# Gated cross attention kernel: three PSUM banks for scores and one for all that follows the turned weights, in place of two and two

## Chip, cores and metric

One core of one Trainium2 chip. The time is the device time of one execution in microseconds (us), the median of the runs shown. Engines are called PE (matrix multiplication), DVE (vector), ACT (scalar), POOL (GpSimd) and SP (here only the queue that issues transfers). PEld is the loading of weights into PE, which can overlap PE's streaming.

## What is computed

A block of a transformer for 32 batches of 100 tokens of width 256, each with its own context of 361 tokens. The change touches only the first half, the cross attention:

```python
Q, K, V = LN(x) @ Wq.T + bq, ctx @ Wk.T + bk, ctx @ Wv.T + bv     # 16 heads of 16
attn = softmax(mask(Q K^T / 4))                                   # 100 x 361 per head
O = concat(attn @ V) @ Wo.T + bo
x = x + tanh(g_xattn) * O
```

The second half (self attention whose values and outputs are mixed from 8 experts per head) follows, and takes 1,320 us of the 1,873.

## The kernel before

The program runs in three stretches. The queries of all batches come first (to 57 us), then the cross attention (57 to 551 us), then the second half. The cross attention is `stage_cross` (L396): each engine has its own program there, with the same frame. `batches` (L82) calls `body(b)` for each of the 32 batches: two written out, 26 in a hardware loop of two batches a turn (even batch first), and four written out at the end. `body` has 16 **steps**, one per head. In each step an engine issues its own work for the step's head, and, lagging behind, work for heads of earlier steps; at the start of a body those are still heads of the batch before (`lagging`, L413). Nothing is reordered at run time: an engine issues in exactly this order, and stops at a wait until the semaphore has the value.

For a head h of batch b:

- PE, step h, `scores` (L887): one matmul of 361 columns into a bank of `c_ps`. It waits until DVE has read the scores that the bank held before (L891).
- DVE, step h, `masked` (L682): adds the mask, writes `c_sm` to SBUF and finds the maximum. L689 is this and its read of the accumulator.
- ACT, step h, `exp` (L800, L805).
- PE, step h+4, `turn` (L895, L899): three transposes into a bank of `c_pt`.
- DVE or (for six heads of 16) ACT, step h+5 or h+4, `copy_ext` (L694, L699; L825, L830): PSUM to SBUF.
- PE, step h+6, for four heads at once, `attend` (L903, L920): 24 products of weights and values. So these come at steps 9 and 13 (heads 0 to 3 and 4 to 7 of this batch) and 1 and 5 (heads 8 to 11 and 12 to 15 of the batch before). They write columns 0 to 199 of a bank of `c_pa`.

Then, for the batch before, in the body of b: DVE `invert` (step 2, L701), POOL `spread` (L598), PE `turn_rden` (step 6, L927: denominators turned into columns 256 to 455 of the same bank of `c_pa`), ACT `copy_rt` (step 7, L809, L812: those columns to SBUF), DVE `normalize` (step 9, L706, L710: sums times denominators into `c_an`), PE `project` (steps 14 and 15, L935, L938: `c_an` times the output weights into columns 0 to 255 of the same bank). And for the batch before that one, DVE `residual` (step 0, L712, L719), `moments` (step 1) and `mean_var` (step 2); SP stores the result. In the last batch `project` stands at steps 11 and 12 (`behind_last`, L965) and the three operations of DVE at steps 12 to 14 (L768). PE also computes keys for two batches ahead (L864; steps 0, 2, 3, 4) and values for the next (L881; steps 6 to 12), in two banks of `c_pp`.

All eight banks of PSUM are used: two each for `c_ps`, `c_pt`, `c_pa` and `c_pp`. The bank of `c_pa` is that of the batch's parity, so sums of one batch collect in one while the batch before is normalized and projected in the other. The only wait for it at `attend` is L909: that `residual` of two batches earlier has read its bank.

Of the kernel before, what the change touches and what calls it, by code (L numbers as in the profile page):

```python
# [395 lines left out]
def stage_cross(nc, k, sems, queries, cross, f, x, ctx_t, mask, q_parts, k_parts, big, mv, x1, sel_t, q_t, k_t):  # L396
# [10 lines left out]
    LAG_T, LAG_C, LAG_E, LAG_A = 4, 5, 4, 6  # L407
    RING = 2 * CLOSE
    RT = 256
    ACT_COPIES = (1, 4, 7, 10, 13, 15)  # L410
    TAIL = 12

# [7 lines left out]
    with ExitStack() as ctx:  # L420
# [15 lines left out]
        an = m.sbuf("c_an", [P, DC * SQ])  # L436
        x1s, xt = (m.sbuf(f"c_x1{n}", [SQ, 2, D]) for n in "st")
        warm = m.sbuf("c_warm", [P, 1])
        p_s = m.psum("c_ps", [P, 2, 512])
        p_t = m.psum("c_pt", [P, 2, 512])  # L440
        p_a = m.psum("c_pa", [P, 2, 512])
        p_p = m.psum("c_pp", [P, 2, 512])
        s_one, s_bvb, s_bo, s_tg = (held.sem(f"c_s_{n}") for n in ("one", "bvb", "bo", "tg"))
        s_ctx, s_kwh, s_kwl, s_kst, s_qst, s_mask, s_x, s_st = (
# [221 lines left out]
        def vector_programs(dve):  # L666
            def bias_values():
                dve.memset(ones[:, :], 1.0).then_inc(s_one, 1)
                dve.wait_ge(s_one, 1)
                dve.wait_ge(queries.s_weights, 48)  # L670
                for c in range(DC):
                    dve.tensor_scalar(bvb[:, c, :], ones[:, :], bvc[:, c:c + 1], None,
                                      ALU.mult).then_inc(s_bvb, 1)

            def key_lo(b, c):
                dve.wait_ge(s_khi, DC * b.n + c + 1)
                at_least(dve, s_kwl[b.par], 16 * b.half)
                dve.scalar_tensor_tensor(out=klo[:, b.par, c, :], in0=p_p[:, c, 0:SK],
                                         scalar=bkc[:, c:c + 1], in1=khi[:, b.par, c, :],
                                         op0=ALU.add, op1=ALU.subtract).then_inc(s_klo, 1)  # L680

            def masked(b, h):  # L682

                if h == 0:
                    dve.wait_ge(s_mb, b.n + 1)
                dve.wait_ge(s_s, XH * b.n + h + 1)
                at_least(dve, s_ex, XH * b.n + h - 3)
                pass_wait(dve, s_pass_dve)
                dve.tensor_tensor_reduce(  # L689
                    out=sm[:, h % 4, :], in0=p_s[0:SQ, h % 2, 0:SK], in1=mbias[:, b.par, :],  # L690
                    scale=-0.25 / WS, scalar=BIG, op0=ALU.add, op1=ALU.min,
                    accum_out=nmax[:, h % 4:h % 4 + 1]).then_inc(s_sm, 1)

            def copy_ext(b, h):  # L694
                if h in ACT_COPIES:
                    return
                dve.wait_ge(s_t, XH * b.n + h + 1)
                at_least(dve, s_pv, XH * b.n + h + 1 - RING)
                dve.tensor_copy(ext[:, h % RING, :], p_t[0:KW, h % 2, 0:KC * SQ]).then_inc(s_extd, 1)  # L699

            def invert(b):  # L701
                dve.wait_ge(s_ex, XH * (b.n + 1))
                at_least(dve, s_rdx, b.n)
                dve.reciprocal(rden[:, :], den[:, b.par, :]).then_inc(s_rd, 1)

            def normalize(b):  # L706
                dve.wait_ge(s_pv, XH * (b.n + 1))
                dve.wait_ge(s_rt, b.n + 1)
                at_least(dve, s_o, b.n)
                dve.tensor_tensor(an[:, :], p_a[:, b.par, 0:DC * SQ], rt[:, :], ALU.mult).then_inc(s_an, 1)  # L710

            def residual(b):  # L712
                dve.wait_ge(s_o, b.n + 1)
                dve.wait_ge(s_xb, b.n + 1)
                if not leaves(b):
                    dve.wait_ge(s_kept, b.n + 1)
                    dve.wait_ge(s_st[b.par], 16 * (b.half + 1))
                    pass_wait(dve, s_pass_dve)
                dve.scalar_tensor_tensor(out=x1_at(b), in0=p_a[0:SQ, b.par, 0:D],  # L719
                                         scalar=k.tanh_g[0:SQ, 0:1], in1=xbias[:, b.par, :],  # L720
                                         op0=ALU.mult, op1=ALU.add).then_inc(s_x1, 1)

            def moments(b):
                dve.wait_ge(s_x1, b.n + 1)
                at_least(dve, s_mv, b.n)
                pass_wait(dve, s_pass_dve)
                dve.bn_stats(st[:, :], x1_at(b)).then_inc(s_bn, 1)

            def mean_var(b):
                dve.wait_ge(s_bn, b.n + 1)  # L730
                if not leaves(b):
                    dve.wait_ge(s_kept, b.n + 1)
                pass_wait(dve, s_pass_dve)
                dve.bn_aggr(moments_at(b), st[:, :]).then_inc(s_mv, 1)

            def start(n):
                if n in (0, 3):
                    for c in range(DC):
                        key_lo(fixed(n // 3), c)
                elif n == 4:  # L740
                    bias_values()
                elif n == 6:
                    dve.wait_ge(s_bo, 1)
                    dve.wait_ge(queries.s_tanh, 1)
                    dve.tensor_scalar(tgbo[:, :], p_p[:, 0, 0:D], k.tanh_g[:, 0:1], None,
                                      ALU.mult).then_inc(s_tg, 1)

            def tail(b, step):
                if step == 0:
                    residual(b)  # L750
                if step == 1:
                    moments(b)
                if step == 2:
                    mean_var(b)

            def body(b):
                for i in range(XH):
                    lagging(b, i, LAG_C, copy_ext)
                    masked(b, i)
                    if i in (3, 5) and later(b, 2):  # L760
                        key_lo(later(b, 2), i // 5)
                    if i == 2 and not is_first(b):
                        invert(b.before())
                    if i == 9 and not is_first(b):
                        normalize(b.before())
                    if has_two_before(b):
                        tail(b.before().before(), i)
                    if is_last(b):  # L768
                        tail(b.before(), i - 12)

            def rest():
                batches(dve, body)
                last = fixed(NB - 1)
                for i in range(XH, XH + LAG_C):
                    lagging(last, i, LAG_C, copy_ext)
                invert(last)
                normalize(last)
                residual(last)
                moments(last)
                mean_var(last)  # L780

            return start, rest

        def scalar_programs(act):
# [24 lines left out]
            def copy_rt(b):  # L809
                act.wait_ge(s_r, b.n + 1)  # L810
                at_least(act, s_an, b.n)
                act.activation(rt[:, :], p_a[:, b.par, RT:RT + DC * SQ], ACT.Copy).then_inc(s_rt, 1)  # L812

            def start(n):
                if n in (0, 3):
# [40 lines left out]
        def tensor_programs(pe):  # L856
# [30 lines left out]
            def scores(b, h):  # L887
                if h == 0:
                    pe.wait_ge(s_kst[b.par], 64 * (b.half + 1))
                    pe.wait_ge(s_qst[b.par], 128 * (b.half + 1))  # L890
                at_least(pe, s_sm, XH * b.n + h - 1)  # L891
                pe.matmul(p_s[0:SQ, h % 2, 0:SK], qst[:, b.par, HEAD[h], :], kst[:, b.par, HEAD[h] // 2, :],  # L892
                          start=True, stop=True).then_inc(s_s, 1)

            def turn(b, h):  # L895
# [7 lines left out]
            def attend(b, h):  # L903
# [2 lines left out]
                first = h - CLOSE + 1  # L906
                if first == 0:
                    pe.wait_ge(s_vz, KC * (b.n + 1))
                    at_least(pe, s_x1, b.n - 1)  # L909
                mine = range(first, h + 1)  # L910
                for by_act in (False, True):
                    copied = [n for n in mine if (n in ACT_COPIES) == by_act]
# [2 lines left out]
                for c in range(KC):  # L915
                    for n in range(first, h + 1):
                        head = HEAD[n]
                        row, col, odd = 32 * (head % XG // 2), SQ * (head // XG), head % 2
                        v = vz[:, b.par, c, head // 2, :, :].rearrange("p a d -> p (a d)")
                        last = pe.matmul(p_a[row:row + 32, b.par, col:col + SQ],  # L920
                                         v[:, XD * odd:XD * odd + 32],
                                         ext[:, n % RING, c * SQ:(c + 1) * SQ],
                                         start=odd == 0 and c == 0, stop=odd == 1 and c == KC - 1)
# [2 lines left out]

            def turn_rden(b):  # L927
                pe.wait_ge(s_rdx, b.n + 1)
                for c in range(DC):
                    src = rdx[:, c * XG:(c + 1) * XG, :].rearrange("p h d -> p (h d)")  # L930
                    last = pe.transpose(p_a[:, b.par, RT + c * SQ:RT + (c + 1) * SQ], src,
                                        k.ident[0:SQ, 0:SQ])
                last.then_inc(s_r, 1)

            def project(b, c):  # L935
                if c == 0:
                    pe.wait_ge(s_an, b.n + 1)
                last = pe.matmul(p_a[0:SQ, b.par, 0:D], an[:, c * SQ:(c + 1) * SQ], wo[:, c, :],  # L938
                                 start=c == 0, stop=c == DC - 1)
                if c == DC - 1:  # L940
                    last.then_inc(s_o, 1)
# [20 lines left out]
            ahead = {0: (2, keys, 0, 0), 2: (2, keys, 0, 1), 3: (2, keys, 1, 0), 4: (2, keys, 1, 1),  # L962
                     6: (1, values, 0, 0), 7: (1, values, 0, 1), 8: (1, values, 1, 0), 10: (1, values, 1, 1), 11: (1, values, 2, 0), 12: (1, values, 2, 1)}
            behind = {6: (turn_rden,), 14: (project, 0), 15: (project, 1)}
            behind_last = {6: (turn_rden,), 11: (project, 0), 12: (project, 1)}  # L965

            def body(b):
                for i in range(XH):
                    scores(b, i)
                    if i in ahead and later(b, ahead[i][0]):  # L970
                        n, work, *args = ahead[i]
                        work(later(b, n), *args)
                    owed = behind_last if is_last(b) else behind
                    if i in owed and not is_first(b):
                        work, *args = owed[i]
                        work(b.before(), *args)
                    lagging(b, i, LAG_T, turn)
                    lagging(b, i, LAG_A, attend)
# [1009 lines left out]
```

## Time and profile before

| | |
|---|---|
| median of 3 runs | 1874.32 us (1874.13 to 1876.52) |
| the profiled execution's own time | 1874.45 us |
| its span, first to last instruction | 1872.7 us |
| PE busy | 1839.2 us (98%) |
| PEld busy | 1136.9 us (61%) |
| DVE busy | 1469.4 us (78%) |
| ACT busy | 1124.4 us (60%) |
| POOL busy | 1067.1 us (57%) |
| granted TensorE clock | 0.997 of full speed |

The 1.7 us between the span and the execution's time lie outside the first and last instruction. The shares are averages over the whole program; the change is in the stretch from 57 to 551 us only. Ends of matmuls are modelled in this profile (a matmul is shown with its whole latency, and the next may start before the shown end), so starts are the numbers to compare.

### The profile page before, as it was taken

How to read it: one execution, taken by the hardware profiler on the slowest of the kernel's cores; microseconds unless marked ns; L12 is line 12 of the kernel's file. 1: busy time of each engine (PE TensorE's matmuls, PEld its weight loads, DVE VectorE, ACT ScalarE, POOL GpSimd, SP SyncE). 2: the span in 40 equal slices, each digit the busy share in tenths (PEclk: the TensorE clock that was granted, in tenths of full speed). 3: DMA queues.
4: the chain of work that ended last, by engine and by line, in shares of the span. 5: the costliest groups of instructions: out<-in, count | busy, mean ns of one | idle time of the engine just before them, and what ended most of it. 6: DMA issues, size and time to landing. Idle time of an engine off the chain costs nothing. (4 is left out here: it accounts for less than half of the span.)

```text
span 1872.7 us, 57738 instructions
## 1 busy us (share of the span) xinstructions
PE 1839.2 (98%) x13454; PEld 1136.9 (61%) x13454; DVE 1469.4 (78%) x4212; ACT 1124.4 (60%) x3581; POOL 1067.1 (57%) x1722
## 2 busy tenths in 40 slices
PE   6999999999989999999999999999999999999998
PEld 4788888888876554444444445555555555555543
DVE  7799999999979725555555566679999999999989
ACT  4799989998975454444444455455555555555543
POOL 4144444466730005666666666666766776767766
PEclk9999999999999999999999999999999999999999
DMA  5555555565414762000000032122222222222201
GB/s 174 154 128 129 131 125 123 124 160 135 119 32 177 279 249 89 28 28 28 14 28 28 28 121 63 55 79 77 69 78 74 67 82 72 68 82 73 68 25 56
DMA packets 161975, 174.24 MB, mean 93 GB/s; under 512 B 49905, under 2 KB 148594, under 8 KB 159858
## 3 DMA queue, kind: packets, MB, share of 16 engines
q1 hardware_dynamic: 159730, 165.05, 30.2%
q0 software_dynamic: 2176, 8.39, 1.2%
q8 instruction: 28, 0.46, 0.1%
q14 instruction: 41, 0.34, 0.1%
HBM read 112.41 MB, written 60.98 MB: 93 GB/s over the span
## 5 line engine op out<-in xcount | busy, mean ns | idle before, releaser
L1608 POOL TENSOR_TENSOR o_side<-o_side,o_tmp 128x256 f32 (+1 forms) x528 | 397.4, 753 | 190.2 <-POOL o_side L1608 73.4
L1369 PE MATMUL e_pv<-e_vw,e_xhi 128*128 (+1 forms) x1600 | 475.9, 379 | 0.0
L1299 ACT ACTIVATE big<-e_pv,gates 128x128 f32<-128x128 f32 x800 | 227.9, 368 | 279.4 <-PE e_pv L1369 277.9
L1736 ACT ACTIVATE o_tmp<-o_py,gates 128x256 f32<-128x256 f32 x528 | 221.9, 474 | 193.1 <-PE o_py L1808 134.1
L805 ACT ACTIVATE c_ex<-c_sm,c_nmax 100x361 f32<-100x361 f32 x512 | 302.4, 594 | 33.4 <-DVE c_nmax L689 22.3
L1808 PE MATMUL o_py<-o_whi,a_chi 128*128 128x512 f16 x800 | 303.9, 380 | 1.1 <-issue 0.6
L1369 PE MATMUL e_pv<-e_vw,e_xlo 128*128 (+1 forms) x800 | 303.2, 379 | 0.0
L1808 PE MATMUL o_py<-o_whi,a_clo 128*128 128x512 f16 x800 | 303.1, 379 | 0.0
L1808 PE MATMUL o_py<-o_wlo,a_chi 128*128 128x512 f16 x800 | 303.0, 379 | 0.0
L689 DVE CUSTOM_DVE_ANT_0 c_sm<-c_ps,c_mbias 100x361 f32<-100x361 f32 x512 | 270.1, 529 | 34.3 <-PE c_ps L892 27.6
L1244 DVE TENSOR_SCALAR e_acc<-e_pv,gates 128x128 f32<-128x128 f32 x400 | 121.8, 346 | 221.4 <-PE e_pv L1369 221.3
L1668 DVE SCALAR_TENSOR_TENSOR o_main<-o_py,gates,o_main 128x256 f32 (+1 forms) x536 | 256.2, 478 | 36.9 <-issue 22.2
L1369 PEld LDWEIGHTS e_pv<-e_vw,e_xhi 128*128 (+1 forms) x1600 | 156.6, 98 | 185.1
L1668 DVE SCALAR_TENSOR_TENSOR o_side<-o_py,gates,o_side 128x256 f32 (+1 forms) x536 | 254.4, 475 | 0.0
L1146 POOL TENSOR_TENSOR big<-big 128x256 f32<-128x256 f32 x200 | 144.6, 723 | 169.8 <-ACT big L1299 169.5
L899 PE MATMUL c_pt<-ident,c_ex 100*121 100x100 f32 x1536 | 237.4, 264 | 1.8 <-DVE c_ext L699 1.1
L899 PEld LDWEIGHTS c_pt<-ident,c_ex 100*121 100x121 f32 x1536 | 219.0, 185 | 16.6 <-issue 2.3
L892 PE MATMUL c_ps<-c_kst,c_qst 128*100 128x361 f16 x512 | 168.3, 329 | 1.3 <-DVE c_nmax L689 0.6
L699 DVE COPY c_ext<-c_pt 121x300 f32<-121x300 f32 x320 | 148.0, 463 | 8.4 <-PE c_pt L899 6.6
L1719 ACT ACTIVATE a_ex<-a_ps,a_mxs 100x100 f32<-100x100 f32 x256 | 84.5, 342 | 103.9 <-DVE a_mxs L1639 97.4
L1369 PEld LDWEIGHTS e_pv<-e_vw,e_xlo 128*128 (+1 forms) x800 | 78.3, 98 | 94.4
L1808 PEld LDWEIGHTS o_py<-o_whi,a_clo 128*128 (+1 forms) x800 | 78.1, 98 | 94.7
(172 smaller groups left out, 3240.1 us busy)
## 6 DMA issues: line engine op xcount, KB each, us to landing
qk<-e_out SPq DMA_DIRECT2D x16, 1600.0 KB, 5.2
c_kst<-k_parts SPq DMA_DIRECT2D x128, 180.5 KB, 3.4
a_q<-qk SPq DMA_DIRECT2D x64, 200.0 KB, 2.4
a_k<-qk SPq DMA_DIRECT2D x64, 200.0 KB, 2.5
v<-e_out SPq DMA_DIRECT2D x20, 640.0 KB, 3.3
a_v<-v SPq DMA_DIRECT2D x64, 200.0 KB
c_ctx<-in_ctx_t SPq DMA_DIRECT2D x32, 361.0 KB, 3.6
e_wst<-in_v_w POOLq DMA_DIRECT2D x8, 1024.0 KB, 8.4
```

The source lines that it names most:

```text
L689: dve.tensor_tensor_reduce(out=sm[:, h % 4, :], in0=p_s[0:SQ, h % 2, 0:SK], in1=mbias[:, b.par, :], scale=-0.25 / WS, scalar=BIG, op0=ALU. ...
L699: dve.tensor_copy(ext[:, h % RING, :], p_t[0:KW, h % 2, 0:KC * SQ]).then_inc(s_extd, 1)
L805: act.activation(ex[:, h % 4, 0:SK], sm[:, h % 4, :], ACT.Exp, scale=-1.0, bias=nmax[:, h % 4:h % 4 + 1], accum_out=den[:, b.par, HEAD[h]: ...
L892: pe.matmul(p_s[0:SQ, h % 2, 0:SK], qst[:, b.par, HEAD[h], :], kst[:, b.par, HEAD[h] // 2, :], start=True, stop=True).then_inc(s_s, 1)
L899: last = pe.transpose(p_t[0:KW, h % 2, c * SQ:(c + 1) * SQ], ex[:, h % 4, c * KW:(c + 1) * KW], k.ident[0:SQ, 0:SQ])
L1146: pool.tensor_tensor(tsum[:, hh, :, :], tmp[:, hh, 0:2, :], tmp[:, hh, 2:4, :], ALU.add).then_inc(s_ts, 1)
L1299: act.activation(tmp[:, hh, e, :], p_v[:, hh, 1, e * PD:(e + 1) * PD], ACT.Copy, scale=gate).then_inc(s_av, 1)
L1369: last = pe.matmul(p_v[:, hh, half, :], a[:, c, bass.ds(t * P, P)], vw[:, bass.ds(col + (w * DC + c) * VW, 512)], start=j == 0, stop=j == ...
L1608: pool.tensor_tensor(side[:, x.t, :], side[:, x.t, :], tmp[:, slot(x, r), j, :], ALU.add).then_inc(s_pool, 1)
L1668: dve.scalar_tensor_tensor(out=into[:, x.t, :], in0=p_y[:, q, j, :], scalar=gate, in1=into[:, x.t, :], op0=ALU.mult, op1=ALU.add).then_inc ...
L1736: act.activation(tmp[:, slot(x, r), j, :], p_y[:, q, j, :], ACT.Copy, scale=gate).then_inc(s_av, 1)
L1808: last = pe.matmul(p_y[:, q, :, :].rearrange("p j d -> p (j d)"), a[:, bass.ds(buf * T + x.t * P, P)], b[:, buf, cut], start=j == 0, stop= ...
```

## The change

`c_ps` gets a third bank and `c_pa` keeps one. Heads go to banks 0, 1, 2, 0, 1, 2, ... and at the end of a batch 0, 1, 2, 1. A score matmul waits for the earlier head with its bank, which is three heads back in most places, two at heads 1 and 15, four at heads 0 and 2. With one bank for all of `c_pa`:

- sums stay in columns 0 to 199 and turned denominators in 256 to 455; the projection moves to columns 256 to 511.
- `attend` of heads 0 to 3 (step 9) waits until `normalize` of the batch before is done (`s_an`); `normalize` moves from DVE's step 9 to its step 8.
- `attend` of heads 8 to 11 (step 1 of the next body) waits until `residual` of the batch before its own is done (`s_x1`). That `residual` stands at step 0 of the same body. `turn_rden` gets the same kind of wait.
- in the last batch, `project` goes back to steps 14 and 15, and DVE's three operations for batch 30 move behind the body, between the last copies.

```diff
+    BANK = (0, 1, 2) * 4 + (0, 1, 2, 1)
+    BACK = tuple(next(d for d in range(1, XH) if BANK[h - d] == BANK[h]) for h in range(XH))
...
-        p_s = m.psum("c_ps", [P, 2, 512])
+        p_s = m.psum("c_ps", [P, 3, 512])
         p_t = m.psum("c_pt", [P, 2, 512])
-        p_a = m.psum("c_pa", [P, 2, 512])
+        p_a = m.psum("c_pa", [P, 512])
...
-                dve.tensor_tensor(an[:, :], p_a[:, b.par, 0:DC * SQ], rt[:, :], ALU.mult).then_inc(s_an, 1)
+                dve.tensor_tensor(an[:, :], p_a[:, 0:DC * SQ], rt[:, :], ALU.mult).then_inc(s_an, 1)
...
-                dve.scalar_tensor_tensor(out=x1_at(b), in0=p_a[0:SQ, b.par, 0:D],
+                dve.scalar_tensor_tensor(out=x1_at(b), in0=p_a[0:SQ, RT:RT + D],
...
-                    if i == 9 and not is_first(b):
+                    if i == 8 and not is_first(b):
                         normalize(b.before())
                     if has_two_before(b):
                         tail(b.before().before(), i)
-                    if is_last(b):
-                        tail(b.before(), i - 12)
...
                 for i in range(XH, XH + LAG_C):
                     lagging(last, i, LAG_C, copy_ext)
+                    tail(last.before(), i - XH)
...
-                at_least(pe, s_sm, XH * b.n + h - 1)
-                pe.matmul(p_s[0:SQ, h % 2, 0:SK], qst[:, b.par, HEAD[h], :], kst[:, b.par, HEAD[h] // 2, :],
+                at_least(pe, s_sm, XH * b.n + h + 1 - BACK[h])
+                pe.matmul(p_s[0:SQ, BANK[h], 0:SK], qst[:, b.par, HEAD[h], :], kst[:, b.par, HEAD[h] // 2, :],
...
                 if first == 0:
                     pe.wait_ge(s_vz, KC * (b.n + 1))
-                    at_least(pe, s_x1, b.n - 1)
+                    at_least(pe, s_an, b.n)
+                if first == 2 * CLOSE:
+                    at_least(pe, s_x1, b.n)
...
             def turn_rden(b):
                 pe.wait_ge(s_rdx, b.n + 1)
+                at_least(pe, s_x1, b.n)
...
-                last = pe.matmul(p_a[0:SQ, b.par, 0:D], an[:, c * SQ:(c + 1) * SQ], wo[:, c, :],
+                last = pe.matmul(p_a[0:SQ, RT:RT + D], an[:, c * SQ:(c + 1) * SQ], wo[:, c, :],
...
-            behind_last = {6: (turn_rden,), 11: (project, 0), 12: (project, 1)}
```

The reads and writes of `c_ps` and `c_pa` that are not shown change their bank index in the same way.

## Rows read from the trace of the kernel before

**Rows 1.** Busy time by stretch: from:to, length, engine busy (x instructions), clock, DMA

```profile
102.00:117.00 15.00, 15.00 (x196) 13.03 (x195) 13.59 (x49) 13.57 (x44) 9.97 (x24) 1.00 0.51 128
525.00:540.00 15.00, 14.30 (x178) 11.88 (x178) 13.33 (x51) 13.34 (x44) 5.98 (x19) 1.00 0.03 8
```

**Rows 2.** Groups of instructions, 72 to 512 us: busy, mean ns | idle before

```profile
L689 DVE CUSTOM_DVE_ANT_0 c_sm<-c_ps,c_mbias 100x361 f32<-100x361 f32 x460 | 243.2, 529 | 30.0 <-PE c_ps L892 23.8 <-issue 0.2
...
L892 PE MATMUL c_ps<-c_kst,c_qst 128*100 128x361 f16 x460 | 151.0, 328 | 0.0
...
L920 PE MATMUL c_pa<-c_ext,c_v 121*32 121x100 f32 x2764 | 83.4, 253 | 0.0
...
L892 PEld LDWEIGHTS c_ps<-c_kst,c_qst 128*100 128x100 f16 x460 | 57.6, 125 | 17.4 <-DVE c_nmax L689 11.5 <-issue 5.9
```

**Rows 3.** Timeline, batch 16, steps 4, 5 and scores of 6, 10: start, length

```profile
304.11 0.32 PE L892 MATMUL c_ps<-c_kst,c_qst 128*100 128x361 f16 x1
...
305.02 0.32 PE L892 MATMUL c_ps<-c_kst,c_qst 128*100 128x361 f16 x1
...
305.57 0.72 PE L920 MATMUL c_pa<-c_ext,c_v 121*32 121x100 f32 x24
...
306.22 0.12 PEld L892 LDWEIGHTS c_ps<-c_kst,c_qst 128*100 128x100 f16 x1 [0.15 <-issue]
...
310.02 0.12 PEld L892 LDWEIGHTS c_ps<-c_kst,c_qst 128*100 128x100 f16 x1 [0.15 <-DVE c_nmax L689]
```

**Rows 4.** Timeline, batch 16, from PE's step 6 to its step 9

```profile
306.92 0.48 PE L899 MATMUL c_pt<-ident,c_ex 100*121 100x100 f32 x3
...
307.52 0.47 DVE L699 COPY c_ext<-c_pt 121x300 f32<-121x300 f32 x1 [0.18 <-PE c_pt L899]
...
308.09 0.32 ACT L812 ACTIVATE c_rt<-c_pa 128x200 f32<-128x200 f32 x1
...
308.36 0.47 DVE L699 COPY c_ext<-c_pt 121x300 f32<-121x300 f32 x1
...
308.74 0.53 DVE L689 CUSTOM_DVE_ANT_0 c_sm<-c_ps,c_mbias 100x361 f32<-100x361 f32 x1
...
309.34 0.54 DVE L689 CUSTOM_DVE_ANT_0 c_sm<-c_ps,c_mbias 100x361 f32<-100x361 f32 x1
...
309.37 0.72 PE L920 MATMUL c_pa<-c_ext,c_v 121*32 121x100 f32 x24
...
309.80 0.36 DVE L710 TENSOR_TENSOR c_an<-c_pa,c_rt 128x200 f32<-128x200 f32 x1
```

**Rows 5.** Timeline, step 1 of PE in batches 16, 17; step 15 between

```profile
301.36 0.48 DVE L719 SCALAR_TENSOR_TENSOR c_x1s<-c_pa,tanh_g,c_xbias 100x256 f32<-100x256 f32 x1
...
301.59 0.72 PE L920 MATMUL c_pa<-c_ext,c_v 121*32 121x100 f32 x24
...
315.08 0.53 DVE L689 CUSTOM_DVE_ANT_0 c_sm<-c_ps,c_mbias 100x361 f32<-100x361 f32 x1 [0.34 <-PE c_ps L892]
...
316.48 0.48 DVE L719 SCALAR_TENSOR_TENSOR c_x1s<-c_pa,tanh_g,c_xbias 100x256 f32<-100x256 f32 x1
...
316.88 0.72 PE L920 MATMUL c_pa<-c_ext,c_v 121*32 121x100 f32 x24
```

**Rows 6.** Timeline, behind the last batch, where PE does wait

```profile
545.94 0.42 ACT L830 ACTIVATE c_ext<-c_pt 121x300 f32<-121x300 f32 x1 [1.04 <-PE c_pt L899]
...
546.51 0.72 PE L920 MATMUL c_pa<-c_ext,c_v 121*32 121x100 f32 x24 [0.60 <-ACT c_ext L830]
...
548.37 0.37 DVE L710 TENSOR_TENSOR c_an<-c_pa,c_rt 128x200 f32<-128x200 f32 x1 [2.11 <-issue]
...
548.79 1.11 PE L938 MATMUL c_pa<-c_w,c_an 128*100 128x256 f32 x4 [1.24 <-DVE c_an L710]
```

**Rows 7.** Timeline, behind the last batch: DVE

```profile
543.30 0.84 DVE L699 COPY c_ext<-c_pt 121x300 f32<-121x300 f32 x2
...
545.63 0.47 DVE L699 COPY c_ext<-c_pt 121x300 f32<-121x300 f32 x1 [1.48 <-PE c_pt L899]
```

More of the change, by code:

```diff
@@ L689, in masked @@
                 dve.tensor_tensor_reduce(
-                    out=sm[:, h % 4, :], in0=p_s[0:SQ, h % 2, 0:SK], in1=mbias[:, b.par, :],
+                    out=sm[:, h % 4, :], in0=p_s[0:SQ, BANK[h], 0:SK], in1=mbias[:, b.par, :],
                     scale=-0.25 / WS, scalar=BIG, op0=ALU.add, op1=ALU.min,
@@ L811, in copy_rt @@
                 at_least(act, s_an, b.n)
-                act.activation(rt[:, :], p_a[:, b.par, RT:RT + DC * SQ], ACT.Copy).then_inc(s_rt, 1)
+                act.activation(rt[:, :], p_a[:, RT:RT + DC * SQ], ACT.Copy).then_inc(s_rt, 1)
             def start(n):
@@ L919, in attend @@
                         v = vz[:, b.par, c, head // 2, :, :].rearrange("p a d -> p (a d)")
-                        last = pe.matmul(p_a[row:row + 32, b.par, col:col + SQ],
+                        last = pe.matmul(p_a[row:row + 32, col:col + SQ],
                                          v[:, XD * odd:XD * odd + 32],
@@ L928, in turn_rden @@
                 pe.wait_ge(s_rdx, b.n + 1)
+                at_least(pe, s_x1, b.n)
                 for c in range(DC):
                     src = rdx[:, c * XG:(c + 1) * XG, :].rearrange("p h d -> p (h d)")
-                    last = pe.transpose(p_a[:, b.par, RT + c * SQ:RT + (c + 1) * SQ], src,
+                    last = pe.transpose(p_a[:, RT + c * SQ:RT + (c + 1) * SQ], src,
                                         k.ident[0:SQ, 0:SQ])
@@ L972, in body @@
                         work(later(b, n), *args)
-                    owed = behind_last if is_last(b) else behind
-                    if i in owed and not is_first(b):
-                        work, *args = owed[i]
+                    if i in behind and not is_first(b):
+                        work, *args = behind[i]
                         work(b.before(), *args)
```

## The prediction

> **What bounds the kernel now.** I first read the busy time by stretch, to see which engine fills the stretch that the change touches. In a slice of 15 us inside the cross attention PE is busy for all 15.00 us, DVE for 13.59 and ACT for 13.57 [rows 1]. As a matmul's shown end is modelled, that alone doesn't prove that PE never waits. So next come the groups of instructions from 72 to 512 us: PE's idle time is 0.0 in front of the scores (L892) and of the sums (L920), while DVE was idle for 30.0 us in front of its masking, of which 23.8 waiting for scores from PE [rows 2]. DVE waits for PE; PE waits for nobody. Last, the timeline of one batch: the scores of steps 4 and 5 start at 304.11 and 305.02, 0.91 us apart [rows 3], and that is only the streaming of what stands between them (one score matmul, three for keys, three transposes). A batch takes 15.3 us on PE, set by PE's own instructions. The thing to carry over: whatever delays PE in this stretch adds to the time, and whatever relieves a wait of PE gains only if there was one.
>
> **The third bank for scores: no gain, 0 us.** It lets PE issue the scores of a head before DVE has read those of two heads back. One row looks like such a wait: PEld is idle for 17.4 us in front of the scores' weights, 11.5 of it put down to DVE's maximum (L689) and 5.9 to "issue" [rows 2]. But each of these gaps is the same 0.15 us whichever name it has, and each stands behind a group of sums: at 306.22 it is "issue", at 310.02 "DVE" [rows 3]. For the latter the masking that had to be done was that of head 8, started at 308.74 and over at 309.27 [rows 4], 0.75 us before the load at 310.02. A wait that had ended 0.75 us earlier holds nothing. The gap belongs to the switch from the narrow 32-column products to a full-width one; the edit doesn't touch it. The instructions are the same in number and size, so nothing is gained or lost by them either. The Trainium skill ("Perfetto Trace Analysis", section "Matmuls") says that independent groups of matmuls should rotate through different banks, so that the copying out of one overlaps the next. By that rule the scores could only gain, and the sums, which stop rotating, must lose; the two effects are weighed here by the rows, and in this kernel the rule speaks against the change.
>
> **The one bank for sums: a wait at step 9.** `attend` of heads 0 to 3 now needs `normalize` of the batch before. PE reaches it at 309.37 [rows 4]. The chain on DVE that leads there starts at PE itself: the transposes of step 6 start at 306.92; DVE, idle for 0.18 us until they are done, copies at 307.52; then come masking 7, the copy at 308.36, masking 8 at 308.74. The next operation behind a masking starts 0.46 us after it (309.34 to 309.80), so `normalize`, now at step 8, starts at 308.74 + 0.46 = 309.20. Its other input, ACT's copy of the denominators, is done by 308.09 + 0.32 = 308.41, so that doesn't hold it. It takes 0.36, to 309.56. From there to a matmul that waits for it: the last batch shows 548.37 + 0.37 = 548.74 and the matmul at 548.79, 0.05 us [rows 6]. So `attend` starts at 309.61 instead of 309.37: **0.24 us** lost. It can't be made up in the next batch, since the chain restarts each time from PE's own step 6; if PE is later, so is DVE. DVE has slack, but it lies in waits for PE, ahead of this chain. 31 batches have the wait: 31 x 0.24 = 7.4 us. Behind the waiting instruction the 24 products and then scores 10 are queued on PE; masking 10 on DVE and then exp on ACT wait for those and shift with them. `normalize` itself only changes places with masking 9: masking 9 goes from 309.34 to about 309.5, and PE asks for the bank of head 9 only at head 12 by the new order; ACT, which takes it next, has slack too (13.57 us busy of 15 [rows 1]). That costs nothing.
>
> **A wait at step 1.** `attend` of heads 8 to 11 now needs `residual`, which DVE issues at its step 0 of the same body. In an even batch `residual` starts at 301.36 and takes 0.48: 301.84, and with 0.05 for the signal 301.89, against 301.59 on PE: 0.30 us lost. In an odd one 316.48 + 0.48 + 0.05 = 317.01 against 316.88: 0.13 us [rows 5]. (DVE arrives later in even ones, which begin a turn of its loop.) Here too DVE comes from a wait for PE: 0.34 us in front of masking 15 at 315.08 [rows 5], so the loss recurs. Bodies 2 to 29 have it: 14 x 0.30 + 14 x 0.13 = 6.0 us. In bodies 30 and 31, without keys, PE has gaps of its own (14.30 us busy of 15 [rows 1]), and I count nothing. The wait of `turn_rden` at step 6 is for the same `residual`, five steps old: 0. Why the wait must be there though the columns differ: the Trainium skill ("PSUM — Partial Sum Buffer", section "PSUM bank collisions raise a hardware error") says that two engines may not be in the same bank and the same 32 partitions at once. No run here shows it; it only tells that the wait can't be dropped.
>
> **The last batch.** The two projections move from steps 11 and 12 to 14 and 15 on PE, and DVE's `residual`, statistics and mean of batch 30 move from steps 12 to 14 to behind the body. There DVE issues two copies at 543.30 and is then idle for 1.48 us until 545.63 [rows 7], which covers the three operations (`residual` takes 0.48 [rows 5], the two others I put at no more each). PE's chain at the end is copies and transposes. If the cover failed, the price would be at most the operations' own time, some 1.4 us. I take 0, between -0.5 and +1.4.
>
> **The sum.** 0 + 7.4 + 6.0 + 0 = 13.4 us on the profiled execution's 1874.45: 1887.9 us, 0.7% slower. The median of the runs is 0.1 below that execution, which changes nothing.
>
> **Bounds of the unknown costs.** No row shows these very waits. The signal takes 0.05 by the nearest row, the same operation of DVE followed by a matmul. The only sum that waits starts at 546.51, after an ACT copy that ends at 545.94 + 0.42 = 546.36: 0.15 us [rows 6]. With 0.15 for all 59 waits the loss grows by 59 x 0.10 = 5.9, to 1893.8. Downwards, records of starts may stand 0.1 us off the true order, which would take 5.9 off: 1882.0.
>
> **The rivals.**
> - *Only one wait bites.* If DVE is ahead of what the rows say at one place (its loop overhead in even batches shrinks, say), 7.4 or 6.0 us stay: 1880.5 to 1881.9. For: the odd gap is only 0.13. Against: both chains are released by PE. Chance 0.08.
> - *Faster: the scores' wait was real.* The place is PE's L892 behind a group of sums. If the gaps named after DVE in rows 2 were true waits on the reading of the bank, the third bank would take 11.5 us off; with the new waits hidden because DVE also gets the scores earlier, 1874.45 - 11.5 = 1863.0; it ends faster as long as the new waits cost under 0.19 us each (11.5 / 59). For: the name in the row. Against: all gaps are alike, and 0.75 us of slack. Chance 0.09. The skill's rule on rotation, read for the scores alone, would give this same time.
> - *No difference.* PE's starts in the trace are where its sequencer lets them go; if PE in truth is some 0.3 us behind the records when it comes to the sums, both waits are hidden: 1874.4. The same comes out if the waits were made without effect. For: PE's ends are modelled. Against: where DVE waits for PE, it starts right behind PE's shown end (306.92 + 0.48 = 307.40, the copy at 307.52 [rows 4]), which ties the records of the two engines together. Chance 0.09.
> - *The forecast*, both waits, 1882 to 1894: chance 0.74.
>
> **How the numbers follow.** 1887.9 is the forecast's own sum. From 1880 to 1894 the range takes the forecast and the first rival (0.82) and leaves out the other two. A change within 0.2% (3.7 us) is about what a measurement of this kernel can't tell from none. Faster 0.09, same 0.09, slower 0.82.
>
> **What would show it.** In the profile after: idle time of PE in front of L920 with the releaser `c_an` L710, some 31 times about 0.24 us, and with L719, some 28 times between 0.13 and 0.30; the batch period 15.7 to 15.8 us in place of 15.3; the PEld gap of 0.15 us in front of L892 still there, as often. DVE's idle in front of its masking grows by what PE loses. The second half is untouched in length. I am wrong if PE's idle in front of L920 stays near 0, if the gaps in front of L892 vanish, or if the waits are twice as long, which would mean that DVE doesn't come from a wait for PE.

## The result and the profile after

The changed kernel takes 1891.31 us (median of 5 runs, 1890.4 to 1891.43) against 1874.51 us (5 runs, 1874.13 to 1877.19) before. The ratio on record is 1.0079, with a 95% interval from 1.0068 to 1.0091: 0.7 to 0.9% slower. (It is not the quotient of the two medians, which is 1.0090 and lies inside the interval; the same holds for the ratios below.)

The head of the page of the changed kernel, its first two parts:

```profile
span 1889.6 us, 57783 instructions
PE 1843.7 (98%) x13454; PEld 1138.0 (60%) x13454; DVE 1468.9 (78%) x4212; ACT 1128.2 (60%) x3581; POOL 1067.7 (57%) x1722
```

The numbers of instructions on the engines are those of before, and so are their busy times to within 5 us. The span grew by 16.9 us, so the time went into gaps. Where they are is told by the groups of instructions of the changed kernel, from 72 to 512 us, which answer to [rows 2]:

```profile
L691 DVE CUSTOM_DVE_ANT_0 c_sm<-c_ps,c_mbias 100x361 f32<-100x361 f32 x446 | 235.7, 528 | 43.5 <-PE c_ps L893 24.0 <-ACT c_ex L806 13.1 <-issue 4.6
...
L893 PE MATMUL c_ps<-c_kst,c_qst 128*100 128x361 f16 x446 | 146.4, 328 | 0.0
...
L923 PE MATMUL c_pa<-c_ext,c_v 121*32 121x100 f32 x2688 | 80.9, 253 | 9.9 <-issue 5.6 <-DVE c_x1s L721 3.2
...
L923 PEld LDWEIGHTS c_pa<-c_ext,c_v 121*32 121x32 f32 x2688 | 56.9, 109 | 23.8 <-issue 9.7 <-DVE c_x1s L721 8.5
...
L893 PEld LDWEIGHTS c_ps<-c_kst,c_qst 128*100 128x100 f16 x446 | 55.9, 125 | 17.0 <-DVE c_nmax L691 8.6 <-issue 8.3
```

PE, which had no idle time in front of the sums before, now has 9.9 us there, and PEld 23.8 (11.3 before, where nothing was waited for). In front of the scores nothing changed: 0.0 for PE, and 17.0 for PEld where [rows 2] had 17.4. The name in that row moved from "DVE" towards "issue" and its sum stayed, which is what a gap looks like that is no wait. DVE's idle time in front of its masking grew from 30.0 to 43.5 us, which is about what PE loses in these batches. The names there say little: 13.1 us stand under ACT's exp here, and 3.5 in run 1 below, with the same total.

The timeline of one batch shows the wait at step 9. These rows of the changed kernel answer to [rows 4]:

```profile
316.39 0.53 DVE L691 CUSTOM_DVE_ANT_0 c_sm<-c_ps,c_mbias 100x361 f32<-100x361 f32 x1
...
316.61 0.48 PE L900 MATMUL c_pt<-ident,c_ex 100*121 100x100 f32 x3
...
316.84 0.36 DVE L712 TENSOR_TENSOR c_an<-c_pa,c_rt 128x200 f32<-128x200 f32 x1
...
317.31 0.33 PE L923 MATMUL c_pa<-c_ext,c_v 121*32 121x100 f32 x5 [0.21 <-issue]
```

`normalize` starts 0.45 us behind masking 8, as foretold. In the kernel before, the sums of this step started 0.41 us behind the start of the transposes, in the same batch:

```profile
308.96 0.48 PE L899 MATMUL c_pt<-ident,c_ex 100*121 100x100 f32 x3
309.37 0.72 PE L920 MATMUL c_pa<-c_ext,c_v 121*32 121x100 f32 x24
```

Here that would be 317.02, and they start at 317.31: 0.29 us lost. Two things are to be learnt from the row. The profile names the releaser "issue", not DVE, although the code has the wait on `s_an` there; and the idle time that it shows, 0.21, is not the loss, since a matmul's shown end is modelled. Starts against starts give the loss.

The wait at step 1, in PE's timeline of the changed kernel, an even batch and the next, odd one:

```profile
308.54 0.46 PE L900 MATMUL c_pt<-ident,c_ex 100*121 100x100 f32 x3
309.24 0.72 PE L923 MATMUL c_pa<-c_ext,c_v 121*32 121x100 f32 x24 [0.24 <-DVE c_x1s L721]
...
324.43 0.46 PE L900 MATMUL c_pt<-ident,c_ex 100*121 100x100 f32 x3
324.94 0.72 PE L923 MATMUL c_pa<-c_ext,c_v 121*32 121x100 f32 x24
```

At this step the distance before was 0.39 us (316.49 and 316.88 in its timeline). So 309.24 - 308.54 - 0.39 = 0.31 us are lost in the even batch, 324.94 - 324.43 - 0.39 = 0.12 in the odd one.

The prediction counted nothing in the last two batches, where no keys are computed. But they wait too. In batch 30 the sums start 530.11 - 529.35 = 0.76 us behind the transposes, where it was 515.71 - 515.25 = 0.46 before:

```profile
529.35 0.53 PE L900 MATMUL c_pt<-ident,c_ex 100*121 100x100 f32 x3
530.11 0.64 PE L923 MATMUL c_pa<-c_ext,c_v 121*32 121x100 f32 x20 [0.23 <-DVE c_x1s L721]
```

The same subtraction for all 128 groups of sums of the two traces gives, in total:

| where | batches | us each | us |
|---|---|---|---|
| step 9 (`normalize`) | 2 to 27 | 0.28 to 0.29 | 7.4 |
| step 9 | 1, 28, 29, 31 | 0.22 | 0.9 |
| step 9 | 30 | 0.49 | 0.5 |
| step 1 (`residual`) | 14 of batches 2 to 29 | 0.29 to 0.38 | 4.5 |
| step 1 | the other 14 | 0.11 to 0.13 | 1.8 |
| step 1 | 30 and 31 | 0.29 and 0.30 | 0.6 |
| steps 13 and 5 | all | 0 | 0.1 |

8.8 us at step 9 and 6.9 at step 1: 15.7 us.

Last, the change is in the first stretch only, so I compare where the second half begins: the first product of `e_pt`. Before, then after (the same lines in the two programs):

```profile
L1331 PE MATMUL e_pt<-ident,big x64: 249/256/397, 552.8 to 570.2; 100*128 100x100 f32 x64
```

```profile
L1333 PE MATMUL e_pt<-ident,big x64: 249/256/400, 568.4 to 586.4; 100*128 100x100 f32 x64
```

It begins 568.4 - 552.8 = 15.6 us later. The first scores start at 57.3 us before and 57.2 after. From there to the second half, which is the cross attention, it is 495.5 us before and 511.2 after: 15.7 us more, and that is what the waits give. Each experiment gives this length beside its time. (The first scores start anywhere from 57.1 to 59.5 us in the profiled executions of this study, with the same work ahead of them, so the start of the second half alone can mislead by up to 2 us. The five that start at 58.3 or later had the granted clock at 0.50 for 3.4 us between 23 and 29 us; in the other eight it stood at 1.00 there.)

The other 1.3 us of the span's growth lie in the second half, whose code is the same. It takes 1319.9 us before and 1321.2 after, and from 1318.0 to 1321.2 over the profiled executions of this study. A part of that is the granted clock. It falls to 0.50, the lower of its two levels (1.2 GHz), around where the second half begins (at 551.5 us before, at 564.9 after, at 562.6 in run 3 below). PE is idle for 1.24 us in front of the last projection there, for `normalize`, and for 2.90 us in front of the second half. How long the clock stays low differs from one execution to the next. The first 20 us of the second half, in the kernel before, the changed kernel and run 3 below (start and end, length, busy time of PE, PEld, DVE, ACT and POOL, clock, DMA):

```profile
552.80:572.80 20.00, 18.94 (x221) 16.88 (x222) 12.29 (x33) 14.56 (x57) 7.25 (x27) 0.86 0.30 107
```

```profile
568.40:588.40 20.00, 18.92 (x218) 17.14 (x219) 11.71 (x33) 14.56 (x57) 7.25 (x27) 0.83 0.29 107
```

```profile
562.40:582.40 20.00, 18.78 (x225) 16.26 (x226) 12.95 (x33) 15.07 (x58) 7.28 (x27) 0.91 0.29 107
```

The second halves of these three take 1319.9, 1321.2 and 1318.8 us.

### The profile page after: what moved, and what is told of

It is laid out like the page before. It is cut to its first block and busy times, and to the rows that moved or that the text cites. A ratio compares the mean times of both kernels' runs of the same rounds, so it can differ in the third digit from the quotient of the medians.

```text
span 1889.6 us, 57783 instructions
## 1 busy us (share of the span) xinstructions
PE 1843.7 (98%) x13454; PEld 1138.0 (60%) x13454; DVE 1468.9 (78%) x4212; ACT 1128.2 (60%) x3581; POOL 1067.7 (57%) x1722
```

## The experiments

All are built on the changed kernel, except where it says otherwise. The kernel before ran beside them on each chip, with medians of 1876.17 us (first four), 1874.85 (next four) and 1876.30 (last three).

**1. Is the third bank worth anything? Two banks for scores.**

```diff
-    BANK = (0, 1, 2) * 4 + (0, 1, 2, 1)
+    BANK = (0, 1) * 8
```

> The changed kernel with scores rotating over two banks only, not three (the third is left unused); one bank for sums as in the changed kernel. My theory (the third bank removes no wait): 1891 us, within 0.1% of the changed kernel, PE's idle in front of the sums as there. Rival (the third bank does bring something, and the new waits cost more than the net shows): slower than 1893 us, with PE idle in front of the scores.

Measured: 1890.08 us (1889.86 to 1890.38), ratio 1.0071 (1.0058 to 1.0085); cross attention 511.7 us. The changed kernel had 1.0079 and 511.2. Taking the third bank away changes nothing that can be measured. The PEld gap in front of the scores stays too:

```profile
L893 PEld LDWEIGHTS c_ps<-c_kst,c_qst 128*100 128x100 f16 x446 | 55.9, 125 | 17.0 <-DVE c_nmax L691 8.7 <-issue 8.3
```

**2. The wait at step 9 alone taken away: `normalize` ahead of masking 8.**

```diff
+                    if i == 8 and not is_first(b):
+                        normalize(b.before())
                     masked(b, i)
...
-                    if i == 8 and not is_first(b):
-                        normalize(b.before())
```

> The changed kernel with normalize issued ahead of masking 8 instead of behind it (DVE step 8). My theory: the wait of the sums at step 9 (0.31 us in the changed kernel) goes, 31 x 0.31 = 9.6 us, so 1881.7 us; the wait at step 1 stays. Rival (a pushed-back masking 8 delays exp and the transposes as much): 1891 us, with a new idle time in front of the transposes or scores.

Measured: 1882.02 us (1880.81 to 1883.92), ratio 1.0031 (1.0019 to 1.0043); cross attention 502.1 us, 9.1 less than in the changed kernel. The 9.6 expected came from a distance of 0.39 us before, where step 9 has 0.41. The sums' starts say that 8.8 us are those of step 9, and that the waits at step 1 lose 0.3 less. In front of the sums, the idle time of PE and PEld that is left is put down to DVE's `residual`:

```profile
L923 PE MATMUL c_pa<-c_ext,c_v 121*32 121x100 f32 x2736 | 82.4, 253 | 4.0 <-DVE c_x1s L721 3.2
...
L923 PEld LDWEIGHTS c_pa<-c_ext,c_v 121*32 121x32 f32 x2736 | 57.1, 109 | 17.1 <-DVE c_x1s L721 8.7
```

The whole "issue" part of the rows of the changed kernel (5.6 and 9.7) is gone, and with it the doubt about what that name stood for: it was the wait for `normalize`.

**3. The wait at step 1 alone taken away: `residual` ahead of masking 0.**

```diff
+                    if i == 0 and has_two_before(b):
+                        residual(b.before().before())
                     masked(b, i)
...
-                    if has_two_before(b):
+                    if i > 0 and has_two_before(b):
                         tail(b.before().before(), i)
```

> The changed kernel with residual issued ahead of masking 0 (DVE step 0). My theory: the wait at step 1 goes (0.31 in even bodies, 0.12 in odd ones, 28 bodies, 6.0 us, and up to 1 us more in the last two), so 1884.3 to 1885.3 us; the wait at step 9 stays. Rival (the wait only moves on to the next step, since masking 0 comes 0.4 us later): 1891 us.

Measured: 1882.95 us (1882.27 to 1885.05), ratio 1.0035 (1.0022 to 1.0049); cross attention 504.1 us, 7.1 less than in the changed kernel, so the 6.0 expected and the "up to 1 us more in the last two". (Its second half starts only 6.0 us sooner than the changed kernel's, but its first scores start 1.1 us later, at 58.3.) The time is below the 1884.3 to 1885.3 expected. In the profiled execution the second half was 2.4 us shorter than in the changed kernel, and 7.1 + 2.4 - 1.1 are the 8.4 us by which the span fell. What is left of PE's idle time in front of the sums is the other part:

```profile
L925 PE MATMUL c_pa<-c_ext,c_v 121*32 121x100 f32 x2712 | 81.6, 253 | 5.8 <-issue 5.5
```

**4. Both.** The edits of 2 and 3 together.

> Both reorderings of DVE together on the changed kernel. My theory (the whole loss is the two waits): 1874.5 to 1876 us, the time before the change, PE idle 0 in front of the sums, and no gain from the third bank. Rival (one bank for sums costs something of its own, or DVE's order matters): over 1878 us; rival (the third bank helps once the waits are gone): under 1872 us.

Measured: 1875.47 us (11 runs, 1874.37 to 1876.14), ratio 0.9994 (0.9985 to 1.0003); cross attention 495.9 us, 0.4 more than before. The kernel is back at the time of before, with one bank for sums:

```profile
L925 PE MATMUL c_pa<-c_ext,c_v 121*32 121x100 f32 x2760 | 83.1, 253 | 0.0
```

The order on DVE shows why. `normalize` now ends 0.28 us before the sums:

```profile
309.29 0.35 DVE L712 TENSOR_TENSOR c_an<-c_pa,c_rt 128x200 f32<-128x200 f32 x1
...
309.92 0.72 PE L925 MATMUL c_pa<-c_ext,c_v 121*32 121x100 f32 x24
```

So one bank for sums costs nothing of its own that can be measured; the two waits were the loss.

**5. Both, with two banks for scores.** The edits of 1 and 4.

> Both reorderings of DVE, and scores over two banks instead of three. My theory (the third bank is worth nothing even where no new wait stands): the time of both_first, 1874 to 1877 us. Rival (the third bank pays once the waits are gone): 2 us or more slower than both_first, with PE idle in front of the scores.

Measured: 1875.58 us (11 runs, 1874.29 to 1877.54), ratio 1.0002 (0.9993 to 1.0011); cross attention 495.7 us. The third bank is worth nothing where no new wait stands either: seven banks do what eight did.

**6. Both, with one bank for scores.**

```diff
-    BANK = (0, 1, 2) * 4 + (0, 1, 2, 1)
+    BANK = (0,) * 16
```

> Both reorderings of DVE, and scores in one bank only. It asks how many banks the scores need. Scores then wait for the masking of the head before, which ends some 1.1 us after those scores started (0.55 to its start, 0.53, and the signal), while a step of PE takes 0.78 to 1.2 us. My theory (the first to second bank is what counts): about 0.15 to 0.35 us lost in 12 of 16 steps, 3 us per batch, 1960 to 1990 us. Rival (PE's order hides even that): under 1880 us.

Measured: 2014.43 us (2 runs), ratio 1.0744 (1.0724 to 1.0763). The direction is right and the size expected was too small: the cross attention takes 633.9 us, 138 more than before. A batch of the loop takes 19.4 us in place of 15.3, so 4.1 more; in the last batch the granted clock was also at 0.50 for 17 us. In this kernel's timeline a step with values, which takes 0.78 us in the changed kernel, takes 1.18:

```profile
301.46 0.12 PEld L895 LDWEIGHTS c_ps<-c_kst,c_qst 128*100 128x100 f16 x1 [0.36 <-DVE c_nmax L691]
...
302.05 0.53 DVE L691 CUSTOM_DVE_ANT_0 c_sm<-c_ps,c_mbias 100x361 f32<-100x361 f32 x1
...
302.64 0.12 PEld L895 LDWEIGHTS c_ps<-c_kst,c_qst 128*100 128x100 f16 x1 [0.36 <-DVE c_nmax L691]
```

From the scores to the masking 302.05 - 301.46 = 0.59 us, the masking 0.53, the signal 0.06: 1.18, not 1.1. In the middle batches no step is shorter than that, so PE loses 0.40 us in those that took 0.78, where I had put 0.35 as the most. This is also what a true wait for a score bank looks like in the groups of this kernel. PE is idle too, and the PEld row has 98.3 us, to be set against the even 17 us of the others:

```profile
L895 PE MATMUL c_ps<-c_kst,c_qst 128*100 128x361 f16 x363 | 129.4, 356 | 39.0 <-DVE c_nmax L691 29.6
...
L895 PEld LDWEIGHTS c_ps<-c_kst,c_qst 128*100 128x100 f16 x363 | 43.9, 121 | 98.3 <-DVE c_nmax L691 97.4 <-issue 0.9
```

**7 and 8. What are the gaps around a group of sums? Eight heads at once.** First on the kernel before, then on the changed kernel (where the second wait has to be told the new group).

```diff
-CLOSE = 4
+CLOSE = 8
...
-                if first == 2 * CLOSE:
+                if first == XH // 2:
```

> The kernel before with the sums of eight heads at once, at steps 13 and 5 only, not of four at steps 9, 13, 1, 5 (and 16 buffers for the copies, not 8). It asks what the gaps around each group of sums are: in front of one PE is 0.09 us late, behind one PEld is idle for 0.15 us, with no waiting shown. My theory (they belong to the change between 32-column and full-width products, not to a wait): half of the groups go, 64 x 0.11 to 0.2 us, so 1862 to 1868 us. Rival (they are waits, or the double burst of 1.3 us starves DVE and ACT): 1875 us or slower.

> The changed kernel (three banks for scores, one for sums) with the sums of eight heads at once, at steps 13 and 5. The waits on normalize (step 8) and residual (step 0) then have four steps or more of slack, so by my theory this has no stall at the sums although the bank is one, and the time of close8_before; if the third bank matters under the double burst, up to some us less than close8_before. Rival (one bank costs something of its own): 10 us or more slower than close8_before.

Measured: 1884.39 us (1883.94 to 1886.32), ratio 1.0052 (1.0038 to 1.0065), and 1880.92 us (1880.21 to 1884.66), ratio 1.0036 (1.0022 to 1.005). Cross attention 508.5 and 502.4 us. What I expected of the time was wrong in both: slower than before, not 6 to 12 us faster. What I expected of the gaps was right. In the second of the two kernels, with half as many groups, PEld's idle time in front of the scores is half of what it was, and the name "DVE" is gone from it:

```profile
L893 PEld LDWEIGHTS c_ps<-c_kst,c_qst 128*100 128x100 f16 x454 | 57.4, 126 | 8.6 <-issue 7.9
```

So the gap goes with the groups of sums. The gain of it was given back by a new wait, in front of the transposes, where PEld had 11.7 us of idle time in the changed kernel:

```profile
L900 PEld LDWEIGHTS c_pt<-ident,c_ex 100*121 100x121 f32 x1363 | 190.0, 185 | 34.7 <-ACT c_ext L831 13.4 <-DVE c_ext L701 8.3 <-issue 1.1
```

While PE is at 48 products in a row, DVE has nothing to mask, and afterwards the copies of ACT and of DVE come too late for the transposes. DVE's and PEld's rows in the timeline of that kernel:

```profile
301.91 0.53 DVE L691 CUSTOM_DVE_ANT_0 c_sm<-c_ps,c_mbias 100x361 f32<-100x361 f32 x1 [0.81 <-PE c_ps L893]
```

```profile
305.29 0.39 PEld L900 LDWEIGHTS c_pt<-ident,c_ex 100*121 100x121 f32 x3 [0.36 <-DVE c_ext L701]
```

And here the waits of the single bank cost nothing, as they have several steps of slack: PE has 0.0 us of idle time in front of its sums, and the changed kernel is even 3.5 us faster than the kernel before, both with eight at once. In the loop a batch takes 15.50 us there against 15.64. (Of the 6.1 us between the two lengths above, a part is the clock: it fell to 0.50 9 us ahead of the second half in the first, 0.6 us ahead in the other.) That pair differs in the number of both kinds of banks, and no run takes the third bank away from the changed kernel with eight at once. Run 11 asks what the bank is worth in the next order only.

**9. The sums one place later: behind the scores of the next step.**

```diff
-    LAG_T, LAG_C, LAG_E, LAG_A = 4, 5, 4, 6
+    LAG_T, LAG_C, LAG_E, LAG_A = 4, 5, 4, 7
...
                     scores(b, i)
+                    lagging(b, i, LAG_A, attend)
...
                     lagging(b, i, LAG_T, turn)
-                    lagging(b, i, LAG_A, attend)
```

> The changed kernel with each group of sums issued one step later, right behind that step's scores (steps 10, 14, 2, 6; DVE's order as in the changed kernel). My theory: normalize (step 8) and residual (step 0) then are a whole step of PE earlier than the sums that wait for them, so both stalls go without any reordering of DVE: 1874 to 1877 us, PE idle 0 in front of the sums. Rival (PE is held elsewhere by the later sums): over 1878 us.

Measured: 1882.5 us (1881.88 to 1883.71), ratio 1.0032 (1.002 to 1.0045); cross attention 504.8 us, 9.2 more than before. Wrong, and the fault is mine: the sums stood at the end of a step, so behind the next step's scores is not a whole step later but one score matmul, 0.16 us. Taking 0.16 off the waits of 0.29 (step 9) and of 0.31 and 0.12 (step 1) leaves 0.13, 0.15 and nothing. In PE's timeline of this kernel, the sums behind the scores of step 2 (the wait for `residual`, even batch) and of step 10 (the wait for `normalize`):

```profile
305.18 0.32 PE L893 MATMUL c_ps<-c_kst,c_qst 128*100 128x361 f16 x1
305.58 0.72 PE L923 MATMUL c_pa<-c_ext,c_v 121*32 121x100 f32 x24
...
313.10 0.32 PE L893 MATMUL c_ps<-c_kst,c_qst 128*100 128x361 f16 x1
313.48 0.72 PE L923 MATMUL c_pa<-c_ext,c_v 121*32 121x100 f32 x24
```

The sums start 0.40 and 0.38 us behind the scores; where nothing waits it is 0.24 or 0.25 (309.30 to 309.54 in the same timeline). So 0.15 and 0.13 us are left, as the one matmul of delay says, and in odd batches the sums of step 2 start 0.25 us behind the scores: no wait. Over all batches 3.9 us are left at step 10 and 2.6 at step 2, 6.5 of the 9.2. Another 1.6 lie behind the last sums: from there to the second half it is 7.9 us (554.03 to 561.96) against 6.3 before (546.51 to 552.79), and the granted clock was at 0.50 for all of it:

```profile
554.00:562.00 8.00, 3.82 (x31) 2.25 (x32) 1.46 (x4) 1.82 (x3) 0.00 (x0) 0.50 0.05 14
```

The last 1.1 us, 0.04 per batch, aren't settled.

The run shows one thing more. With the sums right behind the scores, the PEld gap is gone from the scores and stands in front of what follows the sums now, mostly the values. So it goes with the place of the sums, not with the scores or their bank:

```profile
L893 PEld LDWEIGHTS c_ps<-c_kst,c_qst 128*100 128x100 f16 x453 | 57.4, 127 | 0.0
...
L882 PEld LDWEIGHTS c_pp<-c_whi,c_ctxhi 128*121 128x121 f16 x168 | 22.6, 134 | 8.5 <-issue 8.5
```

**10 and 11. Eight heads at once, behind that step's scores**, with three banks for scores and with two. The edits of 8 and 9, and for the second that of 1.

> The same with the sums of eight heads at once (steps 14 and 6, behind that step's scores). With eight at once the transposes were held by DVE's and ACT's copies, since DVE sat idle for 0.81 us in each burst. Now DVE has a head's scores to mask during the burst. My theory: the burst starves nobody, and the 64 groups saved give 64 x 0.11 = 7 us against the kernel before: 1867 to 1870 us. Rival (DVE, with 13.6 us of work in 15, can't follow uneven steps): 1875 us or slower.

> As ahead8, with scores over two banks and not three. If a third bank is worth anything in this kernel it is where DVE falls behind after a burst. My theory: 1 to 4 us slower than ahead8, as the two kernels with eight sums at once differed by 3.5 us. Rival: the same time.

Measured: 1882.87 us (1881.76 to 1886.79), ratio 1.0039 (1.0025 to 1.0053), and 1890.69 us (1890.47 to 1893.72), ratio 1.0083 (1.0069 to 1.0097). Cross attention 504.1 and 511.1 us. The first is no faster than run 8: one head's scores don't fill a burst of 1.2 us, and the transposes still wait for copies. The second answers the question of the third bank: here it is worth 7.0 us of the cross attention, 7.8 by the medians, and a batch of the loop takes 15.80 us in place of 15.55. Its list of waits (us in total, times, longest) has PEld waiting for DVE in front of the scores, which the first, with three banks, doesn't have:

```profile
PEld c_ps L893 <- DVE c_nmax L691: 5.6, 26, 0.2
PEld c_pp L882 <- DVE c_klo L680: 3.9, 26, 0.2
```

The second of these rows, in front of the values, looks like another cost of the missing bank and is none. With three banks the same gap is there, as long, under the name "issue":

```profile
PEld c_pp L882 <- issue: 4.2, 28, 0.2
```

It stands behind a group of sums in both. I had expected 1 to 4 us; the sign was right and the size too small.

## Why the prediction was right

It said 1887.9 us, from 1880 to 1894; measured are 1891.3. Point by point:

- *What bounds the stretch.* PE, without a wait. The experiments agree: with both waits gone the time is that of before, and nothing done to banks or to the order brought it below that.
- *Third bank: 0 us.* Right, by runs 1 and 5. The reason given, that the row naming DVE in front of the scores shows a fixed gap and no wait, is shown by run 8, where the gap halves with the groups, by run 9, where it moves with them, and by run 6, where a true wait looks different. The faster rival took that row at its word; it fell with these.
- *The wait at step 9: 7.4 us.* The mechanism was right; the size is 8.8 (0.29 instead of 0.24 in most batches). The term that was mis-sized is the signal from DVE to the waiting sums: 0.05 us was taken from `project` behind `normalize` in the last batch. Here it is 317.31 - 317.20 = 0.11 by these rounded rows, and 0.10 in all 31 batches. The upper bound, from the only sum that waits before, was 0.15, so the value lies between the two rows.
- *The wait at step 1: 6.0 us.* In the 28 batches that were counted the waits are 0.31 and 0.12 against 0.30 and 0.13, and make 6.3 us. Here the signal is 0.05 to 0.06. The step that failed, a small one, is to count nothing in the last two: PE's gaps of its own don't cover the wait there, 0.3 us are lost in each. With them it is 6.9, and run 3 took 7.1 off.
- *Last batch: 0.* It wasn't tried by itself. From the sums of its step 9 to its last sums it takes 9.13 us before (537.38 to 546.51), 9.27 in the changed kernel (552.61 to 561.88) and 9.27 also in run 4 without the waits, so moving the work there cost some 0.15 us.
- *The sum.* 13.4 foreseen, 15.7 in the cross attention: 1.4 more at step 9, 0.9 more at step 1. The other 1.1 of the 16.8 us between the medians is within what the second half scatters by, which no term of the sum was for.
- *What to look for.* The idle time in front of the sums, the batch period (15.8 us on average; batches of 15.7 and 15.9 us take turns) and the unchanged gap in front of the scores came as written. Not as written: the wait for `normalize` stands in the profile as "issue", and the one for `residual` is named 16 times in PE's rows, not 28, since a wait of 0.12 us leaves PE no idle time to show.
- *One bite only, no difference.* Runs 2 and 3 show that both waits bite: without them the cross attention is 9.1 and 7.1 us shorter.

That two engines may not be in one bank and the same 32 partitions at once was taken from the Trainium skill ("PSUM — Partial Sum Buffer", section "PSUM bank collisions raise a hardware error") to explain why the waits are there. No run here shows what happens without them.

## What to carry to other kernels

Where one engine is full and waits for nobody, a bank more for what it writes brings nothing, and a bank less costs what the waits cost that replace it. (Runs 10 and 11 are the other case: once that engine does wait for the reader of a bank, the bank counts.) So with a bank less, look for each such wait at what the other engine issues just before, and move that one instruction one place up. Here two such moves on DVE made seven banks as good as eight, and left one bank free. Whether a named wait is one is told by its size: the same length under two names, going with what stands in front, is the engine's own. And where a sum comes out, look at its terms one by one all the same. With 0.39 for 0.41 us at step 9, and nothing for the last two batches, the waits would make 9.6 + 6.0 = 15.6 us, the right total from two wrong terms.

## What was not expected

- A group of products that waits for DVE's `normalize` starts 0.10 us behind its shown end, in all 31 batches; one that waits for `residual`, 0.05 to 0.06, in every batch where it waits. Both are DVE operations in front of the same line of PE's program. Why they differ stays open.
- Half as many switches between narrow and full products made the kernel slower (1.0052 and 1.0036). The transposes then waited for ACT's and DVE's copies. That DVE, which has work for some 13.6 us in every 15, couldn't catch up 0.81 us of idling is a reading of the timeline that no run tries by itself.
- The third bank, worth nothing in the even order, was worth 7.8 us in the uneven one (1882.87 against 1890.69).
